# Audio tower on one core: preparation, output and diagonals laid anew among the 32 places of a group

## What is computed

```python
A = -jnp.exp(A_log)
dbc = jnp.einsum('ble,ce->blc', x, W_dbc)
delta, Bm, Cm = jnp.split(dbc, [DT_RANK, DT_RANK + N_STATE], axis=-1)
delta = jax.nn.softplus(jnp.einsum('blr,er->ble', delta, W_dt) + b_dt)
dA = jnp.exp(delta[..., None] * A)
dBx = (delta * x)[..., None] * Bm[:, :, None, :]
_, hs = jax.lax.associative_scan(combine, (dA, dBx), axis=1)   # a1*a2, h1*a2 + h2
y = jnp.einsum('blen,bln->ble', hs, Cm)
return y + Dp * x
```

## Time and profile before

| | us |
|---|---|
| median of 3 runs (lowest to highest) | 6769.01 (6760.99 to 6769.22) |
| the profiled execution | 6773.74 |
| its span, first to last instruction | 6771.6 |
| TensorE matmul busy | 5095.6 (75%) |
| TensorE weight load busy | 2061.5 (30%) |
| VectorE busy | 6079.0 (90%) |
| ScalarE busy | 4964.5 (73%) |
| GpSimd busy | 5857.8 (87%) |
| mean granted clock of TensorE | 0.852 |

### The profile page before, as it was taken

The page is one execution under the profiler, slowest core; times in us unless marked ns, Lnnn a source line. Parts: engine busy times, 40 slices in busy tenths (PEclk is TensorE's granted clock), DMA queues, the critical chain, the costliest instruction groups (busy, mean ns, idle before and its releaser), DMA issues. The chain is left out here.

```text
span 6771.6 us, 112630 instructions
## 1 busy us (share of the span) xinstructions
PE 5095.6 (75%) x34128; PEld 2061.5 (30%) x34128; DVE 6079.0 (90%) x3973; ACT 4964.5 (73%) x10234; POOL 5857.8 (87%) x932
## 2 busy tenths in 40 slices
PE   6777777777777777777777777777777777775787
PEld 2233233233333323323332222223223222222344
DVE  7999999999999999999999999999999999996543
ACT  6777777778777787787777777777777877874121
POOL 7999999999999999999999998999999999994211
PEclk8888888888888888888888888888888888986888
DMA  6777777777777777777777777777777878874000
GB/s 230 253 252 257 254 257 255 250 254 250 250 253 252 251 259 259 253 255 254 248 250 253 251 244 242 249 242 250 240 251 245 260 257 265 261 253 147 5 7 7
DMA packets 560031, 1561.74 MB, mean 231 GB/s; under 512 B 171954, under 2 KB 318002, under 8 KB 559730
## 3 DMA queue, kind: packets, MB, share of 16 engines
q1 hardware_dynamic: 559858, 1559.96, 70.1%
HBM read 1469.03 MB, written 90.59 MB: 230 GB/s over the span
## 5 line engine op out<-in xcount | busy, mean ns | idle before, releaser
L650 POOL TENSOR_TENSOR u<-u,Bt 128x2976 f32<-128x2976 f32 x896 | 5786.2, 6489 | 393.8 <-DMA u<-dx_rows 392.4
L615 DVE TENSOR_TENSOR_SCAN hT<-decay,u 128x744 f32<-128x744 f32 x3584 | 5799.0, 1682 | 330.0 <-ACT decay L453 307.4
L453 ACT ACTIVATE decay<-decay,a_neg 128x371 f32<-128x371 f32 (+2 forms) x7168 | 3606.2, 556 | 846.7 <-PE decay L296 775.1
L296 PE MATMUL decay<-stk,spread 96*128 96x371 bf16 (+2 forms) x7168 | 1995.0, 368 | 1471.0 <-DVE hT L615 1393.0
L314 PE MATMUL z_bank<-hT,Cst 128*32 128x256 f32 x21504 | 1744.7, 451 | 5.5 <-DVE hT L615 3.0
L296 PEld LDWEIGHTS decay<-stk,spread 96*128 96x128 bf16 x7168 | 458.9, 102 | 3094.0 <-DVE hT L615 2653.9
L462 ACT COPY z_sb<-z_bank 128x512 f32<-128x512 f32 x1344 | 798.6, 594 | 444.1 <-PE z_bank L314 432.4
L314 PEld LDWEIGHTS z_bank<-hT,Cst 128*32 128x32 f32 x21504 | 625.3, 122 | 876.3 <-issue 619.9
L1082 POOL TENSOR_TENSOR wr<-pr 128x744 f32<-128x744 f32 x8 | 14.1, 1759 | 397.2 <-DVE pr L1005 397.2
L385 PEld LDWEIGHTS prep_bank<-tmap,yT 64*128 64x128 f32 x1344 | 223.5, 244 | 105.8 <-issue 105.8
L385 PE MATMUL prep_bank<-tmap,yT 64*128 64x32 f32 (+3 forms) x1344 | 251.0, 329 | 0.0
(11 more groups left out here) (163 smaller groups left out, 2579.4 us busy)
## 6 DMA issues: line engine op xcount, KB each, us to landing
u<-dx_rows SPq DMA_DIRECT2D x3584, 372.0 KB, 4.5
delta_parts<-parts SPq DMA_DIRECT2D x112, 279.0 KB, 8.0
stk<-delta_parts SPq DMA_DIRECT2D x112, 279.0 KB, 5.1
y_rows<-z_sb SPq DMA_DIRECT2D x1792, 12.0 KB
yT<-y_rows SPq DMA_DIRECT2D x112, 192.0 KB, 6.8
dx_rows<-dx SPq DMA_DIRECT2D x112, 186.0 KB, 4.7
xT<-in_x SPq DMA_DIRECT2D x64, 186.0 KB, 5.2
xP<-in_x SPq DMA_DIRECT2D x64, 186.0 KB, 4.1
```

Of the source, the lines that this page charges most:

```text
L296: nc.tensor.matmul(slot[:, e, :, 1:], spread[0:PARTS * QR, TILES_G * q + er // TILES_G, :], src[:, er % TILES_G, :, 1:], start=True, stop= ...
L453: last = nc.scalar.activation(bank, bank, ACT.Exp, scale=a_neg[:, l, c:c + 1])
L615: nc.vector.tensor_tensor_scan(hT[q % 2][:, i * PAIR:(i + 1) * PAIR], pair_slot(p), u[c % RING][:, part * PAIR:(part + 1) * PAIR], 0.0, AL ...
L650: tt(here, here, Bt[buf][:, :].unsqueeze(1).broadcast_to([P, 2 * HALVES * CHUNK, W0]), ALU.mult).then_inc(s_u, 1)
```

## The change

On TensorE the three items of `after` go from places 1, 19, 23 to 0, 17, 19, the sum from 5, 7, 8 to 5, 7, 9, and the steps that take parts off from 13, 16 to 13, 15. The output of `prev`, before in two parts at 27 (D x and two yT blocks) and 29 (four blocks), becomes four: D x at 23, and two blocks each at 25, 27 and 29. On ScalarE v is no longer stored: |v| and relu(v) are read from the bank, with scale and bias, at places 0 and 1; the logarithm goes from 5 to 7, middle from 15 to 13, low from 17 to 15, B from 21 to 17, C from 24 and 25 to 19 and 21, post from 31 to 29. The tile t_v and the semaphore relu_done are gone. On SyncE the 16 diagonals go from steps 9 to 12 (four each) to steps 10 to 14 (3, 4, 3, 3, 3), and the load of yT from step 14 to 15.

```diff
@@ -249,12 +249,12 @@
                         store_h(before)
                     if c == 8 and prev:
                         reload_x(prev)
-                    if 9 <= c < 13 and prev:
-                        for t in range(4 * (c - 9), 4 * (c - 8)):
+                    if 10 <= c < 15 and prev:
+                        for t in range((0, 3, 7, 10, 13)[c - 10], (3, 7, 10, 13, 16)[c - 10]):
                             diagonal(prev, 1 - half, t)
                     if c == 13 and after:
                         store_dx(after, 1 - half)
-                    if c == 14 and prev:
+                    if c == 15 and prev:
                         load_yT(prev)
 
             first = (0, 0)
@@ -347,7 +347,6 @@
                 else:
                     pe.wait_ge(s_ln, n + 1)
                     nc.tensor.matmul(bank, eye[:, :], t_ln[:, :], start=False, stop=False)
-                    pe.wait_ge(s_relu, n + 1)
                     nc.tensor.matmul(bank, eye[:, :], t_relu[:, :], start=False, stop=True).then_inc(s_delta, 1)
 
             def take_off(at, i):
@@ -363,28 +362,31 @@
                     last = nc.tensor.matmul(prep[:, 0:W0], neg_eye[:, :], parts[:, j, :], start=False, stop=(j == i))
                 last.then_inc((s_rest, s_rest2)[i], 1)
 
-            def to_channels(at, after, part):
-
+            def times_D(at, after):
+
+                l, _ = at
+                pe.wait_ge(s_xP, 16 * (G(at) + 1))
+                if after:
+                    pe.wait_ge(s_read, 3 * (G(after) + 1))
+                if pair_mean[l]:
+                    x = xP[:, :].rearrange("p (t two) -> p two t", two=2)
+                    nc.tensor.matmul(prep[:, 0:W0 // 2], d_diag[:, l, :], x[:, 0, :], start=True, stop=False)
+                    nc.tensor.matmul(prep[:, 0:W0 // 2], d_diag[:, l, :], x[:, 1, :], start=False, stop=False)
+                else:
+                    nc.tensor.matmul(prep[:, 0:W0], d_diag[:, l, :], xP[:, :], start=True, stop=False)
+
+            def to_channels(at, part):
                 l, _ = at
                 n = G(at)
                 if part == 0:
                     pe.wait_ge(s_yT, 16 * (n + 1))
-                    pe.wait_ge(s_xP, 16 * (n + 1))
-                    if after:
-                        pe.wait_ge(s_read, 3 * (G(after) + 1))
-                    if pair_mean[l]:
-                        x = xP[:, :].rearrange("p (t two) -> p two t", two=2)
-                        nc.tensor.matmul(prep[:, 0:W0 // 2], d_diag[:, l, :], x[:, 0, :], start=True, stop=False)
-                        nc.tensor.matmul(prep[:, 0:W0 // 2], d_diag[:, l, :], x[:, 1, :], start=False, stop=False)
-                    else:
-                        nc.tensor.matmul(prep[:, 0:W0], d_diag[:, l, :], xP[:, :], start=True, stop=False)
                 w = CG * TB // 2 if pair_mean[l] else CG * TB
                 base = 0 if pair_mean[l] else CG * TB
-                for k in (range(2) if part == 0 else range(2, KB)):
+                for k in range(2 * part, 2 * part + 2):
                     m = w if k < KB - 1 else (W0 - CG * TB * (KB - 1)) * w // (CG * TB)
                     last = nc.tensor.matmul(prep[:, k * w:k * w + m], yT[:, k, :], tmap[:, base:base + m],
                                             start=False, stop=(k == KB - 1))
-                if part == 1:
+                if part == 2:
                     last.then_inc(s_Y, 1)
 
             def body(half, here, prev, before, after):
@@ -396,14 +398,16 @@
                             fill(here, half, q - 1, i // 2 - 1)
                         elif prev:
                             fill(prev, 1 - half, TILES_G - 1, i // 2 - 1)
-                    if after and p in (1, 19, 23):
-                        item(after, 1 - half, (1, 19, 23).index(p))
-                    if after and p in (5, 7, 8):
-                        sum_delta(after, (5, 7, 8).index(p))
-                    if after and p in (13, 16):
-                        take_off(after, (13, 16).index(p))
-                    if prev and p in (27, 29):
-                        to_channels(prev, after, (27, 29).index(p))
+                    if after and p in (0, 17, 19):
+                        item(after, 1 - half, (0, 17, 19).index(p))
+                    if after and p in (5, 7, 9):
+                        sum_delta(after, (5, 7, 9).index(p))
+                    if after and p in (13, 15):
+                        take_off(after, (13, 15).index(p))
+                    if prev and p == 23:
+                        times_D(prev, after)
+                    if prev and p in (25, 27, 29):
+                        to_channels(prev, (25, 27, 29).index(p))
 
             first = (0, 0)
             item(first, 0, 0)
@@ -416,8 +420,9 @@
             layer_bodies(pe, body)
             for i in range(FILLS):
                 fill(LAST, 1, TILES_G - 1, i)
-            to_channels(LAST, None, 0)
-            to_channels(LAST, None, 1)
+            times_D(LAST, None)
+            for i in range(3):
+                to_channels(LAST, i)
 
 
         @block.scalar
@@ -461,13 +466,18 @@
                 src = zb[:, :].rearrange("p (k e t) -> p k t e", k=2, e=EPT)
                 nc.scalar.copy(z_sb[buf][:, 2 * i:2 * i + 2, :, q * EPT:(q + 1) * EPT], src).then_inc(s_zev, 1)
 
-            def take_dt(at):
+            def absolute(at):
                 l, _ = at
-                n = G(at)
-
-                act.wait_ge(s_item, 3 * n + 1)
+                act.wait_ge(s_item, 3 * G(at) + 1)
                 sc, bi = cols[:, 2 * l:2 * l + 1], cols[:, 2 * l + 1:2 * l + 2]
-                nc.scalar.activation(t_v[:, :], prep[:, 0:W0], ACT.Identity, scale=sc, bias=bi).then_inc(s_read, 1)
+                nc.scalar.activation(t_abs[:, :], prep[:, 0:W0], ACT.Abs, scale=sc, bias=bi).then_inc(s_abs, 1)
+
+            def positive(at):
+                l, _ = at
+                if not known_below(G(at), 1):
+                    act.wait_ge(s_delta, G(at))
+                sc, bi = cols[:, 2 * l:2 * l + 1], cols[:, 2 * l + 1:2 * l + 2]
+                nc.scalar.activation(t_relu[:, :], prep[:, 0:W0], ACT.Relu, scale=sc, bias=bi).then_inc(s_read, 1)
 
             def take_B(at, buf):
                 n = G(at)
@@ -488,10 +498,6 @@
                 if b == 1:
                     ins.then_inc(s_read, 1)
 
-            def absolute(at):
-                act.wait_ge(s_read, 3 * G(at) + 1)
-                nc.scalar.activation(t_abs[:, :], t_v[:, :], ACT.Abs).then_inc(s_abs, 1)
-
             def decayed(at):
                 act.wait_ge(s_abs, G(at) + 1)
                 if not known_below(G(at), 1):
@@ -505,10 +511,6 @@
             def logarithm(at):
                 act.wait_ge(s_w, G(at) + 1)
                 nc.scalar.activation(t_ln[:, :], t_w[:, :], ACT.Ln, bias=1.0).then_inc(s_ln, 1)
-
-            def positive(at):
-                act.wait_ge(s_read, 3 * G(at) + 1)
-                nc.scalar.activation(t_relu[:, :], t_v[:, :], ACT.Relu).then_inc(s_relu, 1)
 
             def high(at):
                 n = G(at)
@@ -544,37 +546,37 @@
                             read_z(here, half, q - 1, i // 2 - 1)
                         elif prev:
                             read_z(prev, 1 - half, TILES_G - 1, i // 2 - 1)
-                    if prev and p == 31:
+                    if prev and p == 29:
                         post(prev)
                     if not after:
                         continue
+                    if p == 0:
+                        absolute(after)
                     if p == 1:
-                        take_dt(after)
-                        absolute(after)
+                        positive(after)
                     if p == 3:
                         decayed(after)
-                        positive(after)
                     if p == 5:
                         one_plus(after)
+                    if p == 7:
                         logarithm(after)
                     if p == 9:
                         high(after)
+                    if p == 13:
+                        middle(after)
                     if p == 15:
-                        middle(after)
+                        low(after)
                     if p == 17:
-                        low(after)
-                    if p == 21:
                         take_B(after, 1 - half)
-                    if p in (24, 25):
-                        take_C(after, 1 - half, p - 24)
+                    if p in (19, 21):
+                        take_C(after, 1 - half, (19, 21).index(p))
 
             first = (0, 0)
-            take_dt(first)
             absolute(first)
+            positive(first)
             decayed(first)
             one_plus(first)
             logarithm(first)
-            positive(first)
             high(first)
             middle(first)
             low(first)
```

(4 more changed lines are left out.)

## The result

The changed kernel takes 6572.18 us (median of 4 runs, 6557.59 to 6586.36) against 6769.11 us: a ratio of 0.9709, 95% interval 0.9683 to 0.9735. That is 197 us less, where 73 were forecast: the sign was right, the size was not, by more than a factor of two. The range held the time. The profiled execution of the changed kernel took 6557.59 us with a span of 6555.6, 216 less than the profiled one before: some 14.6 under its own median, where that of before was 4.7 over.

A forecast was written before the change was run, and what follows sets the result against it. VectorE's chain of scans was taken as the bound, with 307.4 us of waits for ScalarE's exponentials to win. Loss falling from 2.8 to 2.15 us a group, 0.65 in 112 groups, is 73 us: 6696 us, range 6530 to 6800.

The forecast's parts named there:

- step 1: TensorE's order: short yT matmuls at place 25 do not keep the clock up; places 26 to 31 cost 1.75 us.
- the low stretch: TensorE at 1.2 GHz from place 25 or 26 on, costing 1.75 us a group at places 26 to 31.
- the long form: Groups whose clock does not rise before the next group; the gain at the late places was forecast to lie here.
- step 2: First item at place 0 instead of 1: costs 0.8 us when the clock is low from place 0, otherwise 0.
- the second fall: TensorE's second clock drop in a group, put down to places 31 and 0, both holding only spreads.
- step 3: ScalarE reads the bank instead of storing t_v: 0.35 us less work a group, worth nothing by itself.
- step 4: SyncE's diagonals and load_yT moved: the wait for z_sb (286.6 us) goes, but no gain is taken.
- rival D: ScalarE's instruction stream shifts stalls at loop turns: +150 us if the first layer gets them, -50 if the second loses them; chance 0.08.
- A: Rival: place 25 counts as busy and the clock stays up from 23 to 30; 6500 to 6545 us; chance 0.16 including nearby.
- B: Rival: nothing changes, the low clock lasts from place 25 into the next group every time; 6755 to 6780 us; chance 0.16.
- C: Rival: slower by the item at place 0, costing 1.5 us instead of 0.8 in every group; 6842 us; chance 0.10.

The follow-up runs named there:

- experiment 2: The changed kernel with four short fp32 matmuls of 32 columns added at place 24, result unread: 6504.16 us, ratio 0.9619.
- experiment 10: The kernel before with idle fills (matmuls whose result nobody reads) at places 24, 25 and 31: 6560.51 us, ratio 0.9697.
- experiment 12: The changed kernel with the first item still at place 0, but Abs and Relu both at place 1 on ScalarE: 6634.36 us, ratio 0.9811.
- experiment 8: The changed kernel with the 16 diagonals again in four steps (9 to 12) and the load of yT at step 14: 6562.33 us, ratio 0.9726.
- experiment 7: The changed kernel with v stored again: copy at place 0, Abs at place 1, Exp and Relu at place 3: 6600.28 us, ratio 0.9779.
- experiment 6: The changed kernel with the first item back at place 1 and both ScalarE reads of it at place 1: 6686.2 us, ratio 0.9906.
- experiment 1: The changed kernel with one idle fill (16 matmuls of 256 columns, result unread) added at place 24: 6444.26 us, ratio 0.9524.
- experiment 3: The changed kernel with idle fills (matmuls whose result nobody reads) at places 24 and 31: 6423.85 us, ratio 0.9491.

## Why the prediction was right or wrong

*The clock still falls at places 24 and 25* (step 1): right. The clock is 0.50 from 2348.8 to 2362.4, from place 25 on. Its reason was half right: experiment 2 gives half of the effect to short matmuls.

*What the low stretch costs* (step 1): the mechanism and its size were right. TensorE in the changed kernel, at 1.2 GHz:

```profile
2352.56 0.80 PE L296 MATMUL decay<-stk,spread 96*128 96x371 bf16 x2
2353.29 1.06 PE L387 MATMUL prep_bank<-tmap,yT 64*128 64x32 f32 x4
2354.28 0.80 PE L296 MATMUL decay<-stk,spread 96*128 96x371 bf16 x2
2355.02 1.94 PE L314 MATMUL z_bank<-hT,Cst 128*32 128x256 f32 x16
2356.89 0.80 PE L296 MATMUL decay<-stk,spread 96*128 96x371 bf16 x2
...
2361.20 1.45 PE L296 MATMUL decay<-stk,spread 96*128 96x371 bf16 x4
2362.49 0.79 PE L332 MATMUL prep_bank<-xT,w_dt_rows 128*128 128x372 f32 x2
```

A yT place takes 1.72 us (forecast 1.7) and a fill place 2.61 (2.6); the first wait is ahead of scan 29, as forecast, and both waits with their restarts make 0.72 + 1.09 = 1.81 us (1.75). The term was mis-sized only in how often it comes: 116.8 us in 112 groups is 1.04 a group, where 0.75 x 1.75 = 1.31 stood in the sum. 0.27 x 112 = 30 us. The gain was in the long form, as forecast: 28 groups before lost over 3 us at these places, and none does now.

*The start of the group* (step 2): this is the step that failed. I put 0.8 us on the new start where the clock is low, and counted that in all groups. It is 0.5 us where the clock is low at place 0 from the start, 0.34 over all with a low start, and most starts are at the full clock: 0.12 us a group, 13.4 us in all instead of 0.8 x 112 = 90. That is 76 us, the largest part of the miss. Two readings led there. I took "it often reaches into the next group" from the long form of before; now the low stretch ends at 2362.4, and the item of the next place 0 begins at 2362.49, at the full clock. And I gave the second fall to places 31 and 0, which the change leaves, and did not ask what an item between the two light places does: the share of groups with a low start went from 60 to 24 of 61.

*ScalarE* (step 3): "worth nothing by itself" was wrong for place 1. I took the 0.6 us that ScalarE is free in each place as cover everywhere, but at places 0 and 1 it is not: these wait for the scan just before, as step 2 itself says. Two operations at place 1 cost 0.37 to 0.39 us at the full clock (experiments 10 and 12), and experiment 12 is 62 us slower for them (69 by the ratios). High waits for the last sum as forecast (97.4 us in 108, 0.9 each, forecast 0.5), and nobody waits for it.

*SyncE* (step 4): right. It brought nothing (experiment 8). load_yT now waits for the last diagonals, 106.8 us in 110, and yT lands in 4.2 us instead of 6.8.

*The turn of the loops* was rival D, which as a chance stood for slower, but named -50 us if the second layer's loop lost its stalls. That is what happened, and the sum left it out: the gap after scan 31 fell by 43.6 us, from 67.2 to 23.6. In the second layer's loop it was 5.1 us at a turn; now one of the longest is

```profile
4057.94 4.90 DVE L617 TENSOR_TENSOR_SCAN hT<-decay,u 128x744 f32<-128x744 f32 x3 [1.93 <-PE z_bank L314]
```

The first layer's loop has no such gap in either kernel. ScalarE's time with nothing to wait for ahead of its exponentials, 34.2 us in 15 times before, is gone in the changed kernel, and a part is back in experiment 7:

```profile
ACT decay L459 <- issue: 17.5, 7, 3.0
```

Experiment 7 has one more operation of ScalarE in each group, and its turns cost 29 us more; experiments 6 and 12 only move operations, and there the gaps after scan 31 stay at 33 and 29 us in all. So the number of ScalarE's instructions, as rival D had it, is the likelier cause, which is not shown; why only these loops have it was not tried.

*The sum, term by term,* against the table of lost time. Of before I had 2.8 x 112 = 314 us, read from the first layer's loop; the table has 357.2, and the 44 more are about the turns of the other loops, which I did not keep apart. Of the changed kernel I had 2.15 x 112 = 241 us; it is 144.8: 30 less for the stretch, 76 less for the start, 24 more for the end of the group, which had no term, and 14 less for small gaps and rounding. Together 44 + 96 = 140 us, and 212 - 73 = 139.

*The rivals.* The time fell into the part that the chances gave to A and what lies near it (0.16), but by another way: the clock was low at places 24 to 30, as forecast. A was wrong for this change, but experiments 1 and 3 show what it would have brought: 6444 and 6424 us. B and C did not come. C's place was right, its sign was not.

## What to carry to other kernels

Where a resource is taken in turn and the count does not divide the ring (here 32 places on 3 slots), find the places without slack first, and price every operation of every engine there, at both clocks; slack read off the other places does not hold. A sum that mixes two waits in one number per group can't be checked; lay the lost time by place before forecasting. And when a matmul engine off the critical path dips to the low clock, work that nobody needs, put at the light places, shows in one run what the dips are worth; here it was 148 us on top of the change.

## What the runs showed of the hardware

- The clock of TensorE fell after a stretch with 2.44 us of matmuls in 3.29 us, 1.60 of them of 32 columns (experiment 2), and did not fall where an idle fill of 256 columns, 1.07 us instead of 0.97, stood in the place of the short ones (experiment 1). It also fell after a pause of 2.71 us (2327.09 in experiment 1).
- A fill place took TensorE 2.6 us at 1.2 GHz, and fits into the 1.6 us of a scan at 2.4 GHz; four yT matmuls 1.06 (2353.29 above) and 0.63 us (2326.60 in experiment 2).
- Relu and Abs of a bank with scale and bias cost as much as the copy did: 667 and 673 ns against the 663 of t_v.
